# The last tile's second feed-forward in two halves of 256 tokens, the first between the blocks of the one ahead of it

## The reference

```python
def ffn(x, k0, k1, k2, s0, s1, s2):          # weights are +1 or -1, from boolean matrices
    h = concatenate([x, -x], axis=-1)        # 256
    h = relu(s0 * (h @ sign(k0))) * 2        # 512
    h = relu(s1 * (h @ sign(k1))) * 2        # 512
    return s2 * (h @ sign(k2))               # 128

def attn(x, ...):                            # 16 heads of 8
    Q, K, V = x @ Wq.T + bq, x @ Wk.T + bk, x @ Wv.T + bv
    ctx = softmax(Q @ K.T / sqrt(8)) @ V
    return layernorm(ctx + x) * gamma + beta

x = x + 0.5 * ffn(layernorm(x))
x = x + attn(layernorm(x))
x = x + 0.5 * ffn(layernorm(x))
```

## Time and profile before

| | us |
|---|---|
| median of 3 runs | 772.38 |
| the runs | 767.18, 772.38, 772.47 |
| the profiled execution: its own time | 771.31 |
| its span, first to last instruction | 769.0 |
| mean granted TensorE clock, as a share of full | 0.969 |

### The profile page before, as it was taken

How to read it: one execution, slowest core, us unless ns; L and a number is a source line. 1 busy time by engine, 2 the same in 40 slices (tenths; PEclk the granted TensorE clock), 3 DMA queues, 4 the chain that set the end, 5 groups by cost and what they waited for, 6 DMA issues and landing times.

```text
span 769.0 us, 18471 instructions
## 1 busy us (share of the span) xinstructions
PE 696.8 (91%) x7260; PEld 333.4 (43%) x7260; DVE 647.7 (84%) x1272; ACT 511.3 (66%) x736; POOL 358.4 (47%) x642
## 2 busy tenths in 40 slices
PE   7778696999999999999999999999999998887878
PEld 3433243444444444444445444444445444343424
DVE  6686787898989989898989999898989997777765
ACT  3334666777777777777777777777777776666742
POOL 6420416356464746355464746365463744244320
PEclk9898797999999999999999999999999999899998
DMA  3100110010102020110101010110201010010000
GB/s 79 49 8 29 36 43 23 29 43 11 64 16 64 16 64 17 42 37 2 64 15 64 17 64 16 43 36 3 65 15 64 16 50 17 29 38 2 16 1 27
DMA packets 29508, 25.62 MB, mean 33 GB/s; under 512 B 4336, under 2 KB 29424, under 8 KB 29424
## 3 DMA queue, kind: packets, MB, share of 16 engines
q1 hardware_dynamic: 27664, 23.61, 9.5%
q10 hardware_dynamic: 1760, 0.85, 0.4%
HBM read 5.05 MB, written 4.19 MB: 12 GB/s over the span
## 4 chain that ended last, share of the span: by engine, by line
PE 54%; DVE 23%; ACT 4%; issue 2%; POOL 2%; POOLq 0%; DVEq 0%
DVE row_max L1408 11%; PE ps_z L675 11%; PE ps_z L676 10%; PE ps_c L840 8%; PE ps_s L789 7%; DVE ffn_lo L1287 6%; PE ps_m L763 3%; PE ps_m L852 2%; PE ps_z L657 2%; PE ps_z L686 2%; ACT probs L1070 2%; PE ps_z L688 2%; PE ps_m L774 2%; ACT ffn_hi L1032 1%; DVE k_lo L1399 1%
## 5 line engine op out<-in xcount | busy, mean ns | idle before, releaser
L1408 DVE TENSOR_REDUCE row_max<-ps_s 128x4 f32<-128x1024 f32 x256 | 312.1, 1219 | 58.1 <-PE ps_s L789 57.4
L1070 ACT ACTIVATE probs<-ps_t,score_scale 128x1024 f32<-128x1024 f32 x252 | 280.1, 1112 | 71.7 <-PE ps_t L802 69.4
L1032 ACT ACTIVATE ffn_hi<-ps_z 128x512 f16<-128x512 f32 x261 | 149.6, 595 | 85.4 <-PE ps_z L676 69.9
L675 PE MATMUL ps_z<-ffn_hi,w 128*128 128x512 f16 x464 | 178.1, 384 | 0.1
L676 PE MATMUL ps_z<-ffn_lo,w 128*128 128x512 f16 x464 | 177.0, 381 | 0.0
L1287 DVE SCALAR_TENSOR_TENSOR ffn_lo<-ps_z,ffn_hi 128x512 f16<-128x512 f32 x232 | 155.4, 680 | 9.0 <-ACT ffn_hi L1032 7.3
L840 PE MATMUL ps_c<-probs,v_cols 128*32 128x256 f32 x2048 | 134.3, 391 | 1.3 <-ACT probs L1070 0.7
L789 PE MATMUL ps_s<-k_rows,q_rows 32*128 32x256 f16 x1024 | 102.2, 278 | 27.9 <-DVE row_max L1408 27.4
L802 PE MATMUL ps_t<-q_rows,k_rows 32*128 32x256 f16 x992 | 98.6, 277 | 0.0
L840 PEld LDWEIGHTS ps_c<-probs,v_cols 128*32 128x32 f32 x2048 | 57.7, 111 | 55.9 <-issue 29.0
L789 PEld LDWEIGHTS ps_s<-k_rows,q_rows 32*128 32x128 f16 x1024 | 29.1, 92 | 119.3 <-DVE row_max L1408 59.6
(11 more groups left out here) (212 smaller groups left out, 1088.0 us busy)
## 6 DMA issues: line engine op xcount, KB each, us to landing
x<-L_attn_x SPq DMA_DIRECT2D x16, 256.0 KB, 2.7
q_rows<-q_hi SPq DMA_DIRECT2D x32, 128.0 KB, 2.5
y<-x SPq DMA_DIRECT2D x16, 256.0 KB, 2.1
k_rows<-k_hi SPq DMA_DIRECT2D x30, 128.0 KB, 2.1
q_rows<-no_max SPq DMA_DIRECT2D x16, 128.0 KB, 2.1
q_rows<-q_lo SPq DMA_DIRECT2D x16, 128.0 KB, 2.1
k_rows<-k_lo SPq DMA_DIRECT2D x15, 128.0 KB, 2.1
q_rows<-max_rows SPq DMA_DIRECT2D x64, 8.0 KB
```

The source lines that it names most:

```text
L675: pe.matmul(o[:], w, ffn_hi[:, 1 + k, :], start=(k == 0), stop=False)
L1032: a_.activation(ffn_hi[:, use, :], ps_z[use % 2][:], ACT.Relu if use else ACT.Copy, scale=1.0 if use else XN_SCALE).then_inc(z_hi, 1)
L1070: a_.activation(probs[n % PROBS][:, j:j + 2, :], o[:], ACT.Exp, scale=score_scale[:, 0:1]).then_inc(s_exp, 1)
L1408: v.tensor_reduce(row_max[hb % 2][:].rearrange("p (a l) e -> p l a e", a=2)[:, j:j + 2, :, g % 2], ps_s[:].rearrange("p l (a k) -> p l a k ...
```

## The change

Tile 15's second feed-forward becomes two, A for rows 0 and 1 (its first sequence) and B for rows 2 and 3. Each has banks and semaphores of its own and takes half of the columns of each bank (`solo_columns`). A has slots of its own for its second layer in `ffn_hi` and `ffn_lo` (`solo_slot`). Every operation of a half is half as wide: 256 columns in place of 512 in splits, rests, `solo_in` and `solo_mid`, two rows in place of four elsewhere. The number of instructions on the halves doubles except for those that went row by row.

The order changes on every engine. A's statistics are taken before the contexts of the second sequence are there. Its first layer stands between tile 14's k = 2 and k = 3 blocks of `solo_mid`, its second layer (now block by block of output chunks, `mid_a`) between tile 14's output blocks, and B's first layer in among them. B's second layer alternates with A's output. SyncE stores tile 15 as two DMAs of 128 KB from `x0`, where it was one of 256 KB from `x3`.

```diff
 SOLO_BANKS = (("z0", "z1", "s0", "s1", "z0", "t0", "t1", "c", "m", "z1"),
               ("z0", "z1", "z0", "z1", "z0", "s0", "s1", "t0", "t1", "z1"),
-              ("z0", "c", "m", "z0", "c", "s0", "s1", "t0", "t1", "z1"),)
-SOLO_IN_WAITS = ((1, 1, 1, 1), (1, 1, 2, 3), (1, 1, 1, 2),)
-SOLO_FIRST, SOLO_BEFORE_LAST, SOLO_LAST = 0, 1, 2
+              ("z0", "c", "m", "z0", "c", "s0", "s1", "t0", "t1", "z1"),
+              ("m", "z0", "c", "m", "z0", "s0", "s1", "t0", "t1", "c"),)
+SOLO_IN_WAITS = ((1, 1, 1, 1), (1, 1, 2, 3), (1, 1, 1, 2), (1, 1, 1, 2),)
+SOLO_ROWS = (range(0, TT), range(0, TT), range(0, TT // 2), range(TT // 2, TT))
+SOLO_FIRST, SOLO_BEFORE_LAST, SOLO_LAST_A, SOLO_LAST_B = 0, 1, 2, 3
 
 
...
-        ffn_lo = sb("ffn_lo", [P, 9, TILE], F16)
+        ffn_hi = sb("ffn_hi", [P, 9 + KC, TILE], F16)
...
         ps_c = bank("ps_c")
         ps_m = bank("ps_m")
+        def solo_slot(n, use):
+
+            return use + KC if n == SOLO_LAST_A and use > KC else use
+
+        def solo_columns(n):
+
+            return slice(P * SOLO_ROWS[n].start, P * SOLO_ROWS[n].stop)
+
         solo_banks = {"z0": ps_z[0][:], "z1": ps_z[1][:], "s0": ps_s[:, 0, :], "s1": ps_s[:, 1, :],
                       "t0": ps_t[:, 0, :], "t1": ps_t[:, 1, :], "c": ps_c[:], "m": ps_m[:]}
...
             place_max(L, L_PAR, 3)
             sp.wait_ge(q_lo[SOLO_BEFORE_LAST], Z_USES)
             store_x3(start_of(T - 2))
-            sp.wait_ge(q_lo[SOLO_LAST], Z_USES)
-            store_x3(start_of(T - 1))
-            sp.wait_ge(s_out, 16 * TILES)
+            for b, n in enumerate((SOLO_LAST_A, SOLO_LAST_B)):
+                sp.wait_ge(q_lo[n], Z_USES)
+                sp.dma_start(tile_rows(out_flat, start_of(T - 1))[:, b], x0[:, 2 * b:2 * b + 2, :]).then_inc(s_out, 16)
+            sp.wait_ge(s_out, 16 * (TILES + 1))
 
 
...
+            solo_deviation(SOLO_LAST_A)
             pool.wait_ge(t_mv, 2 * L + 2)
             inverse_deviation(tail_rs, tail_ve, tail_mv, 2, t_rs, 4 * L + 2)
-            solo_deviation(SOLO_LAST)
+            solo_deviation(SOLO_LAST_B)
 
 
         @block.tensor
...
                 pe.wait_ge(q_lo[n], SOLO_IN_WAITS[n][m])
-                w, o = w0[:, m * P:(m + 1) * P], solo_bank(n, 1 + m)
-                pe.matmul(o, w, ffn_hi[:, 0, :], start=True, stop=False)
-                pe.matmul(o, w, ffn_lo[:, 0, :], start=False, stop=True).then_inc(q_full[n], 1)
+                w, c = w0[:, m * P:(m + 1) * P], solo_columns(n)
+                o = solo_bank(n, 1 + m)[:, c]
+                pe.matmul(o, w, ffn_hi[:, 0, c], start=True, stop=False)
+                pe.matmul(o, w, ffn_lo[:, 0, c], start=False, stop=True).then_inc(q_full[n], 1)
 
...
-            for k in range(1, KC):
-                for m in range(KC):
-                    solo_mid(n, k, m)
-            n = SOLO_LAST
-            solo_transpose(n)
-            solo_out(n - 1, 0)
-            solo_out(n - 1, 1)
-            solo_in(n, 0)
+            for m in range(KC):
+                solo_mid(n, 1, m)
+            a, b = SOLO_LAST_A, SOLO_LAST_B
+            pe.wait_ge(q_lo[n], 5)
+            solo_transpose(a)
+            for m in range(KC):
+                solo_mid(n, 2, m)
+            solo_in(a, 0)
             pe.wait_ge(m_free, L_USE + 2)
-            solo_in(n, 1)
-            solo_out(n - 1, 2)
-            solo_out(n - 1, 3)
-            solo_in(n, 2)
-            solo_in(n, 3)
+            solo_in(a, 1)
+            solo_in(a, 2)
+            for m in range(KC):
+                solo_mid(n, 3, m)
+            solo_in(a, 3)
+
+            def mid_a(m):
+
+                pe.wait_ge(q_lo[n], 6 + m)
+                for k in range(KC):
+                    solo_mid(a, k, m)
+
+            def mid_b(m):
+
+                pe.wait_ge(q_lo[a], 6 + m)
+                for k in range(KC):
+                    solo_mid(b, k, m)
+
+            solo_out(n, 0)
+            pe.wait_ge(q_lo[a], 3)
+            solo_transpose(b)
+            mid_a(0)
+            solo_out(n, 1)
+            mid_a(1)
+            pe.wait_ge(q_lo[a], 5)
+            solo_in(b, 0)
+            solo_in(b, 1)
+            solo_out(n, 2)
+            mid_a(2)
+            solo_out(n, 3)
+            mid_a(3)
+            solo_in(b, 2)
+            solo_in(b, 3)
+            mid_b(0)
+            pe.wait_ge(q_lo[n], Z_USES)
+            solo_out(a, 0)
+            solo_out(a, 1)
+            mid_b(1)
+            solo_out(a, 2)
+            mid_b(2)
+            solo_out(a, 3)
+            mid_b(3)
             for k in range(KC):
-                for m in range(KC):
-                    solo_mid(n, k, m)
-            for k in range(KC):
-                solo_out(n, k)
+                solo_out(b, k)
 
 
         @block.scalar
...
             context_copy(L, 7)
+            a, b = SOLO_LAST_A, SOLO_LAST_B
+            for use in range(4):
+                solo_split(a, use)
             for use in range(5, 9):
                 solo_split(n, use)
-            n = SOLO_LAST
-            for use in range(9):
-                solo_split(n, use)
+            solo_split(a, 4)
+            solo_split(b, 0)
+            solo_split(a, 5)
+            solo_split(a, 6)
+            solo_split(b, 1)
+            solo_split(b, 2)
+            solo_split(a, 7)
+            solo_split(a, 8)
+            for use in range(3, 9):
+                solo_split(b, use)
 
...
             solo_split(n, 2)
             for use in range(2, 5):
                 solo_rest(n, use)
+            a, b = SOLO_LAST_A, SOLO_LAST_B
+            dve.wait_ge(s_x2, 2 * L + 1)
+            solo_stats(a, x2[L_PAR], solo_bn, solo_mv)
             context_den(L, 1, L_USE + 1)
             context_norm(L, 1)
             dve.wait_ge(m_free, L_USE + 2)
-            dve.wait_ge(s_x2, 2 * L + 1)
             v.tensor_tensor(att_y[:], ctx_n[:], xn_bv[L_PAR][:, 2:4, :], ALU.add).then_inc(s_y, 1)
             tail_stats(L, 1)
             dve.wait_ge(t_bn, 2 * L + 2)
             mean_var(tail_bn, tail_mv, 2, t_mv)
+            dve.wait_ge(q_full[n], 1)
+            solo_norm(a, x2[L_PAR])
+            solo_rest(a, 0)
             dve.wait_ge(t_rs, 4 * L + 4)
             vec_step(scale_rows(tail_n, att_y, tail_mv, tail_rs, 2))
             vec_so_far()
...
             vec_so_far()
             v.tensor_tensor(x2[L_PAR][:, 2:4, :], tail_g[:], x1_beta[L_PAR][:, 2:4, :], ALU.add).then_inc(s_x2, 1)
             dve.wait_ge(s_x2, 2 * T)
-            solo_stats(x2[L_PAR], solo_bn, solo_mv)
-            dve.wait_ge(q_full[n], 1)
-            solo_norm(SOLO_LAST, x2[L_PAR])
+            solo_stats(b, x2[L_PAR], solo_bn, solo_mv)
+            solo_rest(a, 1)
             solo_rest(n, 5)
+            solo_rest(a, 2)
+            dve.wait_ge(q_full[a], 1)
+            solo_norm(b, x2[L_PAR])
+            solo_rest(a, 3)
+            solo_rest(a, 4)
             solo_rest(n, 6)
-            solo_rest(n + 1, 0)
+            solo_rest(b, 0)
             solo_rest(n, 7)
+            solo_rest(a, 5)
             solo_rest(n, 8)
-            solo_rest(n + 1, 1)
+            solo_rest(a, 6)
+            solo_rest(b, 1)
+            solo_rest(b, 2)
             solo_residual(n, x2[T % 2], x3, stored=T - 2)
-            n = SOLO_LAST
-            for use in range(2, 9):
-                solo_rest(n, use)
-            solo_residual(n, x2[L_PAR], x3, stored=T - 1)
+            solo_rest(a, 7)
+            solo_rest(a, 8)
+            solo_rest(b, 3)
+            solo_rest(b, 4)
+            solo_rest(b, 5)
+            solo_rest(b, 6)
+            solo_residual(a, x2[L_PAR], x0)
+            solo_rest(b, 7)
+            solo_rest(b, 8)
+            solo_residual(b, x2[L_PAR], x0)
 
 
 NAMES = ["L0_attn_x", "L0_attn_Wq", "L0_attn_bq", "L0_attn_Wk", "L0_attn_bk", "L0_attn_Wv", "L0_attn_bv",
```

More of the change, by code:

```diff
@@ L712, in solo_transpose @@
                 pe.wait_ge(q_xn, n + 1)
-                for i in range(TT):
+                for i in SOLO_ROWS[n]:
                     last = pe.transpose(solo_bank(n, 0)[:, i * P:(i + 1) * P], ffn_xn[:, i, :], ident[:])
@@ L718, in solo_in @@
                 pe.wait_ge(q_lo[n], SOLO_IN_WAITS[n][m])
-                w, o = w0[:, m * P:(m + 1) * P], solo_bank(n, 1 + m)
-                pe.matmul(o, w, ffn_hi[:, 0, :], start=True, stop=False)
-                pe.matmul(o, w, ffn_lo[:, 0, :], start=False, stop=True).then_inc(q_full[n], 1)
+                w, c = w0[:, m * P:(m + 1) * P], solo_columns(n)
+                o = solo_bank(n, 1 + m)[:, c]
+                pe.matmul(o, w, ffn_hi[:, 0, c], start=True, stop=False)
+                pe.matmul(o, w, ffn_lo[:, 0, c], start=False, stop=True).then_inc(q_full[n], 1)
             def solo_mid(n, k, m):
                 pe.wait_ge(q_lo[n], 2 + k)
-                w, o = w1[:, k, m * P:(m + 1) * P], solo_bank(n, 5 + m)
-                pe.matmul(o, w, ffn_hi[:, 1 + k, :], start=(k == 0), stop=False)
```

(33 more changed lines are left out.)

15 lines of the change are left out of this document (9 added, 6 removed).

## The result

| | before | after |
|---|---|---|
| median, us | 771.31 | 765.05 |
| lowest and highest of 11 runs each | 766.72, 773.72 | 764.01, 767.19 |
| the profiled execution: time, span | 771.31, 769.0 | 764.93, 763.1 |

The ratio of the times is 0.9933, with a 95% interval of 0.9914 to 0.9952: the change gives 0.5 to 0.9%, 3.7 to 6.6 us. An unchanged time lies outside the interval, though the gain is under the 1% named at the start. The ratio is not that of the medians (765.05 / 771.31 = 0.992); the means, 765.34 and 770.48, give 0.993.

What follows compares the result with a forecast made beforehand. Bound: the chain of waits at the end, with TensorE idle 3.52 us, then at half clock. A 3.5 us gain gave 767.8 from the profiled 771.31, or 768.9 by the median; predicted 768.3, between the two, range 763.7 to 771.6.

Steps and rivals of the forecast that it cites:

- Where the kernel waits, and what fills it: Before tile 15's feed-forward TensorE idles 3.52 us; A's statistics and root hide in idle time, tile 14's blocks fill in.
- The walk through the queues: All five queues followed through the new order from the last attention steps; last residual ends at 762.9 instead of 766.4.
- The prices: Half-width durations in tile 15: VectorE operation from PSUM 0.42 us, ScalarE 0.38, 256-column matmul every 0.109, B's residual 0.49.
- The rival of dearer matmuls: Half-width matmuls on TensorE from 750 cost more than half; at 0.158 each the gain is gone, at 0.216 775.5; chance 0.04.
- the 98 ns: Estimated cost of a 256-column matmul by the skill's page; the gain would be 0.9 us and the time 770.4.
- The clock: TensorE's clock, at 0.52 behind the old idle stretch, stays full in the new order; 1.7 us of the gain.
- (1 - 0.52) x 3.5: Loss on 3.5 us of queued TensorE work at about half speed behind the idle stretch: 1.7 us.
- The sum for the new end: TensorE from 742.82 on: work 16.4 us plus waits 3.0, together 19.4, up to 762.2.
- the earlier pause of 1.19: TensorE idle before 732.06 with granted clock 1.00, taken as sign that new waits of at most 1.3 us keep it full.
- A transfer of 128 KB lands in 2.1 us like one of 256 KB, so the 2.6 us at the end stay.: Last store of tile 15: halving its size leaves the 2.6 us after the last residual unchanged.
- The waits as a sum: TensorE's new waits from 742.82 on: 1.26 + 0.55 + 0.58 + 0.43 + 0.22 = 3.0 us, each counted at full length.
- The split of the gain: Of 3.5 us at the kernel's end, 1.7 is the clock, 0.5 the idle stretch, the rest the shorter end.

Runs made afterwards that it cites:

- clock kept: Kernel before, with 14 unused 512-column matmuls added on TensorE ahead of tile 15's transpose; median 769.41 us, ratio to before 0.9984.
- half a block first: Changed kernel, with A's transpose behind two of the four products of tile 14's k = 2 block; median 765.44 us, ratio to before 0.9937.
- B early: Changed kernel, with B's third and fourth first-layer products, splits and rests ahead of A's last ones; median 765.88 us, ratio to before 0.9933.
- its copy: Kernel before, run again with no edit; median 771.6 us, ratio to before 1.0005.
- one store: Changed kernel, with tile 15 stored by one 256 KB DMA after both residuals; median 766.55 us, ratio to before 0.9946.
- the copy of the changed kernel: Changed kernel, run again with no edit; median 765.81 us, ratio to before 0.9929.
- Halves late: Changed kernel without A's early start, A coming after the attention's last layer norm and tile 14's second layer; median 769.68 us, ratio 0.9999.

## Why the prediction was right, point by point

- **Where the kernel waits, and what fills it.** Right. A's statistics and root were hidden (root done at 739.54, A's scaling from 741.43, when VectorE was through with the attention's statistics), and TensorE had tile 14's blocks and A's in what was one pause.
- **The walk through the queues.** It gave 762.9 - 741.3 = 21.6 us from `den` to the last residual's end; measured 21.55, with the pauses where they were put: 1.3 said and 1.02 listed before A, 0.55 and 0.49 before B, 0.58 and 0.39 inside B's first block, 0.43 and 0.27 before the last output block. A listed pause begins at the end of the last matmul's drain. Counted from starts, as the walk did, the first is 742.15 - 740.97 = 1.18 and the last 760.07 - 759.59 - 0.06 = 0.42.
- **The prices.** A matmul of 256 columns 0.109 (said 0.109), a rest 0.418 (0.42), a split 0.384 (0.38), the half residual 0.484 (0.49). The rival of dearer matmuls is out, and with it, for this kernel, the 98 ns that I had estimated from the Trainium skill (TensorE: Matmul & The Clock Gate, Back-to-back issue gap).
- **The clock.** Right that it stays full; the fall was priced at 1.7 and is worth 1.35, by the run with the clock kept. The step that failed in size is "(1 - 0.52) x 3.5": it took all that TensorE did at half speed to be on the path, where up to tile 15's first product TensorE waited for VectorE at either clock. The sum for the new end does not use this term, so it was not touched. The reason given for the full clock was thinner than it looked: the row that ends at 733.00 stops 0.9 us behind the earlier pause of 1.19, and the fall that was to be excluded came 1.4 us behind its pause. The trace goes on at 1.00 up to 737.
- **"A transfer of 128 KB lands in 2.1 us like one of 256 KB, so the 2.6 us at the end stay."** Wrong. The row for 128 KB was one of `k_rows`, which goes from one place in the on-chip memory to another; a store of that size to `y` lands in 1.7. The end is 0.5 us shorter.
- **The waits as a sum.** The total was right (19.4 us said from TensorE's arrival ahead of A's transpose to its last matmul, 19.3 measured), the value of each part was not: half a block first shows the wait before A to be worth nothing, B early shows that inside B's first block to be worth 0.6.
- **The split of the gain.** Its parts do not add up to 3.5 as they are named. With 1.7 for the clock and 0.5 for the pause, 1.3 are left for the shorter end, and half a split, half a rest and half a residual are 0.21 + 0.26 + 0.26 = 0.73. The total came from the walk and stands without the split; that it was met does not confirm these parts, of which only the clock was measured.
- **The size.** The gain was said to be 3.5 and is 4.0 in the profile, the store being the difference. The median moved by 6.3 us and the ratio by 0.67%, 5.2 us. 4.0 us lie inside the interval (3.7 to 6.6). Whether the 1.2 us between are chance, or falls of the clock ahead of the changed place that come less often in the changed kernel, stays open. Of the ten profiles four had the fall near 693 (before, its copy, clock kept, one store), which are all three of the old order and one of seven of the new; two of the other six (the copy of the changed kernel, B early) had one near 706 instead. Halves late, whose profile is 0.2 us longer from `den` on than that of before, shows no such extra in its ratio of 0.9999, but its interval (0.9978 to 1.0019) would hold 1.2 us.
- The predicted time, 768.3, was 3.2 us too high: 0.5 for the store, 0.5 because it started from 771.8 where the median of more runs of before is 771.31, and 2.2 by which the medians moved further than the profiles' 4.0 (1.2 by the ratio).

## What to carry to other kernels

Where the end of a kernel waits for a short chain on other engines (a layer norm, a root, a scaling), ask what part of the next work needs only data that is there already; taking half of it early filled most of a 3.5 us pause, while the same halves started late won nothing. A long pause of TensorE can cost more than its own length: here the clock behind it cost another 1.35 us, which came back when the pause was broken up. A wait is worth its length only if nothing else holds the next step for as long: before filling one, look at what that step would then wait for (here a full VectorE, and behind it a root on GpSimd), and read a walk's sum as a whole, not as prices of single waits.

## What the runs showed of the hardware

- The clock fell to half behind pauses of 3.52 and 2.58 us, and did not behind ones of 1.02 and 0.49. With the pause of 3.52 filled by idle work it stayed full. But near 693 us it fell for 3.4 us in the run with one store, where TensorE had been busy for 1.16 of the 2.9 us before, and not in the changed kernel, whose compute is the same. That fall cost 1.56 us, the one behind the pause 1.35, the one near 706 us 0.84 and 0.87. `den` lay at 738.98 to 740.21 in the four profiles with a fall at neither 693 nor 706, at 740.46 to 741.68 in the four with that near 693, and at 742.62 and 742.81 in the two with that near 706, in which two earlier falls were longer too.
- Stores to `y`: 128 KB land 1.7 us after their issue and 256 KB 2.1, while a 128 KB copy within the on-chip memory takes 2.1 (median of 30).
- A matmul of 256 columns with a weight load of its own starts every 0.109 us, twice as often as one of 512 (0.216), so that twice as many matmuls of half the width took TensorE no longer.
